# Reading the convolution's transposed value from PSUM, and the inverse root of the norms as one GpSimd power

## The reference

```
x = x + tanh(g_xattn[0]) * conv_mix(layernorm(x), ctx)      # stage A
x = x + tanh(g_ffn[0])   * moe_ffn(layernorm(x))            # stage B
x = x + tanh(g_xattn[1]) * attention(layernorm(x), ctx)     # stage C
x = x + tanh(g_ffn[1])   * lora_moe_ffn(layernorm(x))       # stage D

layernorm(x) = (x - mean(x)) / sqrt(var(x) + 1e-5)

# conv_mix, with v = layernorm(x), 16 heads of 8 rows each:
kv  = v[i] * ctx[j]                  # all 8 x 8 pairs of rows of a head
y   = causal_conv(kv, k[head]) + kv * bias
out = sum over i of y[i, j] * ctx[i]
```

## Time and profile before

| | us |
|---|---|
| median of 3 runs | 895.25 |
| lowest and highest of them | 890.1, 895.4 |
| the profiled execution, its whole time | 886.02 |
| its span in the trace | 884.3 |
| PE busy in the span | 787.3 |
| DVE busy | 618.5 |
| ACT busy | 319.5 |
| POOL busy | 171.2 |

### The profile page before, as it was taken

How to read it: one execution, slowest core, us unless ns; L and a number is a source line. 1 busy time by engine, 2 the same in 40 slices (tenths; PEclk the granted TensorE clock), 3 DMA queues, 4 the chain that set the end, 5 groups by cost and what they waited for, 6 DMA issues and landing times.

```text
span 884.3 us, 13802 instructions
## 1 busy us (share of the span) xinstructions
PE 787.3 (89%) x4627; PEld 629.2 (71%) x4627; DVE 618.5 (70%) x1196; ACT 319.5 (36%) x515; POOL 171.2 (19%) x185
## 2 busy tenths in 40 slices
PE   2887879699999999999997999976699999999994
PEld 2565657478888888888885455535588878888884
DVE  5999999754575466457546888897446785877764
ACT  2120212033333342342233777756143323334221
POOL 1999989700000000003000121211010000000000
PEclk9999999999999999999999999998589999999998
DMA  7221212000000000000101112110000000000000
GB/s 274 72 71 61 75 47 65 13 1 1 1 1 0 0 0 0 0 0 20 31 1 44 51 54 85 53 42 13 0 1 1 1 24 0 0 24 0 24 1 25
DMA packets 22133, 26.06 MB, mean 29 GB/s; under 512 B 5328, under 2 KB 17744, under 8 KB 21968
## 3 DMA queue, kind: packets, MB, share of 16 engines
q1 hardware_dynamic: 22096, 25.60, 9.2%
HBM read 23.22 MB, written 2.10 MB: 29 GB/s over the span
## 4 chain that ended last, share of the span: by engine, by line
PE 67%; DVE 20%; issue 8%; ACT 3%; POOL 1%; DVEq 1%; DMA 1%; SPq 0%; ACTq 0%; POOLq 0%
PE bank L1592 21%; PE bank L1460 19%; PE bank L1473 11%; PE bank L1523 2%; DVE A L864 2%; DVE A L875 2%; PE bank L1513 2%; DVE small L1071 1%; PE bank L1376 1%; PE bank L1601 1%; PE bank L1533 1%; DVE A L1081 1%; PE bank L1510 1%; PE bank L1377 1%; PE bank L1378 1%
## 5 line engine op out<-in xcount | busy, mean ns | idle before, releaser
L1592 PE MATMUL bank<-R 128*128 128x512 f32 (+3 forms) x1080 | 214.9, 360 | 11.4 <-DVE R L1235 4.9
L1592 PEld LDWEIGHTS bank<-R 128*128 128x128 f32 (+1 forms) x1080 | 180.8, 190 | 45.0 <-DVE R L1235 5.1
L1460 PE MATMUL bank<-R 128*128 128x512 f32 x768 | 186.2, 392 | 1.9 <-issue 1.9
L1460 PEld LDWEIGHTS bank<-R 128*128 128x128 f32 x768 | 140.4, 188 | 29.3 <-issue 2.2
L1019 DVE TENSOR_TENSOR A<-bank,A 128x512 f32<-128x512 f32 (+1 forms) x68 | 47.1, 692 | 113.1 <-PE bank L1460 110.8
L1473 PEld LDWEIGHTS bank<-R 128*128 128x128 f32 (+1 forms) x816 | 105.8, 190 | 10.5 <-issue 4.0
L1473 PE MATMUL bank<-R 128*128 128x256 f32 (+1 forms) x816 | 109.4, 284 | 2.5 <-DVE R L1029 2.2
L579 ACT ACTIVATE A<-bank 128x512 f32<-128x512 f32 (+1 forms) x68 | 40.6, 597 | 189.2 <-PE bank L1460 181.5
L1376 PE MATMUL bank<-A 128*128 128x256 f32 x128 | 45.1, 436 | 25.8 <-DVE A L864 17.6
L451 POOL TENSOR_TENSOR A<-A 128x256 f32<-128x256 f32 x64 | 64.1, 1001 | 10.3 <-DVE A L875 10.3
L1376 PEld LDWEIGHTS bank<-A 128*128 128x128 f32 x128 | 21.8, 202 | 44.7 <-DVE A L864 24.9
(11 more groups left out here) (172 smaller groups left out, 1129.4 us busy)
## 6 DMA issues: line engine op xcount, KB each, us to landing
A<-in_w SPq DMA_DIRECT2D x16, 384.0 KB, 3.0
A<-in_w SPq DMA_DIRECT2D x8, 480.0 KB, 3.6
A<-in_ctx_one SPq DMA_DIRECT2D x8, 272.0 KB, 3.6
A<-in_ctx_half SPq DMA_DIRECT2D x8, 256.0 KB, 3.1
A<-in_ctx_nat SPq DMA_DIRECT2D x4, 512.0 KB, 3.7
A<-in_ctx_t SPq DMA_DIRECT2D x128, 16.0 KB, 2.0
out<-X SPq DMA_DIRECT2D x4, 512.0 KB, 2.9
A<-in_filt SPq DMA_DIRECT2D x1, 1536.0 KB, 11.8
```

Of the source, the lines that this page charges most:

```text
L1460: mm = nc.tensor.matmul(dst[0:pr], wX[:, j, at + k * P:at + k * P + pr], mX[:, k], start=(n == 0), stop=(n == 5))
L1592: mm = nc.tensor.matmul(dst, a, m, start=start and n == 0, stop=stop and n == len(prods) - 1, skip_group_check=skip)
```

## The change

1. **The transposed value stays in PSUM.** `a_turned` and vT are gone. a_kv reads TV itself. TV is now two PSUM tiles, bank[2] for even and bank[1] for odd groups, and WB shares bank[3] with OB. The transposition of group g+1 therefore waits for the multiplications of group g-1, the block sums wait for an earlier a_finish, and a_sum waits for a_skip.
2. **The kv ring has four buffers instead of two (KVS), and a_kv runs three heads ahead instead of two (AHEAD).** PE puts three convolutions of the next group ahead of a_sum instead of two.
3. **The inverse root is made by POOL.** After bn_aggr, POOL adds epsilon (128x4 or 128x12) and raises to the power -0.5 in one instruction each. DVE waits for `rs_ready`, multiplies the gain in where there is one (one instruction), and makes nb. The guess and the Newton rounds are gone.
4. **a_skip** of the next group comes at head 11 instead of at head 16.
5. The group loops of stage A on DVE and PE are written out instead of run as hardware loops.

```diff
-TURN_A, BIAS_A = 6, 8
+TURN_A, BIAS_A, SKIP_A = 6, 8, 11
+AHEAD, KVS = 3, 4
...
-        TV, WB, OB = bank[1], bank[2], bank[3]
+        TV, OB = [bank[2], bank[1]], bank[3]
+        WB = OB
...
+            def inverse_root(seen, rs, mv):
+                pool.wait_ge(var_ready, seen)
+                root.mark(nc.gpsimd.tensor_tensor(rs, mv[:, :, 1], eps[:].to_broadcast([P, rs.shape[1]]), ALU.add))
+                pool.wait_ge(root_step, root.value())
+                nc.gpsimd.tensor_tensor(rs, rs, minus_half[:].to_broadcast([P, rs.shape[1]]), ALU.pow).then_inc(rs_ready, 1)
...
+            def a_adds(g, norm):
                 for c in range(CH - len(SPLIT_AT)):
                     split_low(g, c)
                 for h in range(NH0):
                     a_add(g, h)
+                    if norm and h == NORM_A + 3:
+                        inverse_root(BG * (g + 3), rs[:], mv)
                     if h in SPLIT_AT:
                         split_low(g, CH - len(SPLIT_AT) + SPLIT_AT.index(h))
+            for g in range(2):
+                inverse_root(BG * (g + 1), rs[:], mv)
...
+            start = root.value()
+            with pool.Fori(0, G - 1) as g:
+                root.enter(g, 1, start)
+                inverse_root(BG * (G + 2) + BG * g, rs[:], mv)
+            root.leave(1, G - 1, start)
...
+            inverse_root(2 * B + B - BG, crs[:, 0:B - BG], cmv[:, 0:B - BG])
+            inverse_root(3 * B, crs[:, B - BG:], cmv[:, B - BG:])
...
+            split_low1(G - 1, 0)
+            inverse_root(4 * B - BG, drs[:, 0:B - BG], dmv[:, 0:B - BG])
+            split_low1(G - 1, 1)
+            inverse_root(4 * B, drs[:, B - BG:], dmv[:, B - BG:])
...
-            def a_turned(g, first=False):
-                act.wait_ge(vtp_ready, g + 1)
-                if not first:
-                    act.wait_ge(kv_ready, NH0 * g)
-                for k in range(DT):
-                    nc.scalar.activation(vT[:, k * BG:(k + 1) * BG, :], TV[:, k * NT:(k + 1) * NT], ACT.Copy
-                                         ).then_inc(vT_ready, 1)
...
                     step.mark(nc.vector.bn_stats(st[:, i, :], x(i)))
-                    return
-                i -= n
-                if i == 0 or i > n:
+                elif i == n:
                     dve.wait_ge(dve_step, step.value())
-                if i == 0:
-                    step.mark(nc.vector.memset(scrap[:], 0.0))
-                elif i <= n:
-                    step.mark(nc.vector.bn_aggr(mv[:, i - 1, :], st[:, i - 1, :]))
-                elif i == n + 1:
-                    step.mark(nc.vector.tensor_scalar(ve, mv[:, :, 1], EPS, None, ALU.add))
-                elif i == n + 2:
-                    step.mark(nc.vector.tensor_scalar(rs.bitcast(I32), ve.bitcast(I32), 1, None,
-                                                      ALU.logical_shift_right))
-                elif i == n + 3:
-                    step.mark(nc.vector.tensor_scalar(rs.bitcast(I32), rs.bitcast(I32), -1, RSQRT_GUESS,
-                                                      ALU.mult, ALU.add))
-                elif i < n + 4 + 4 * NEWTONS:
-
-                    newton, part = divmod(i - n - 4, 4)
-                    if part == 0:
-                        step.mark(nc.vector.tensor_tensor(tmp, rs, rs, ALU.mult))
-                    elif part == 1:
-                        step.mark(nc.vector.tensor_tensor(tmp, tmp, ve, ALU.mult))
-                    elif part == 2:
-                        step.mark(nc.vector.tensor_scalar(tmp, tmp, -0.5, 1.5, ALU.mult, ALU.add))
-                    elif newton == NEWTONS - 1 and gain is not None:
-                        step.mark(nc.vector.scalar_tensor_tensor(out=rs, in0=rs, scalar=gain, in1=tmp,
-                                                                 op0=ALU.mult, op1=ALU.mult))
+                    nc.vector.memset(scrap[:], 0.0)
+                elif i < 2 * n + 1:
+                    i -= 1
+                    nc.vector.bn_aggr(mv[:, i - n, :], st[:, i - n, :]).then_inc(var_ready, 1)
+                elif i == 2 * n + 1 and gain is not None:
+                    dve.wait_ge(rs_ready, turn)
+                    step.mark(nc.vector.tensor_scalar(rs, rs, gain, None, ALU.mult))
+                else:
+                    if gain is None:
+                        dve.wait_ge(rs_ready, turn)
                     else:
-                        step.mark(nc.vector.tensor_tensor(rs, rs, tmp, ALU.mult))
-                else:
+                        dve.wait_ge(dve_step, step.value())
...
-                u = h % 2
+                u = h % KVS
                 t0 = h * I0
                 c = ctxT[:, h // 8, :, t0 % 64:t0 % 64 + I0]
+                v = TV[g % 2][:].rearrange("p (q t) -> p q t", t=P)
 
                 if not first:
-                    dve.wait_ge(y_ready, 1 + NH0 * g + h - 1)
+                    dve.wait_ge(y_ready, 1 + NH0 * g + h - AHEAD)
                 nc.vector.tensor_tensor(
-                    kv[:, u], vT[:, :, t0:t0 + I0].unsqueeze(3).to_broadcast([P, 8, I0, I0]),
+                    kv[:, u], v[:, :, t0:t0 + I0].unsqueeze(3).to_broadcast([P, 8, I0, I0]),
                     c.unsqueeze(2).to_broadcast([P, 8, I0, I0]), ALU.mult).then_inc(kv_ready, 1)
...
-                    if more and h == NH0:
+                    if more and h == SKIP_A:
...
-            with dve.Fori(0, G - 2) as g:
-                step.enter(g, per, start)
+            for g in range(G - 2):
...
-                if not first:
-                    pe.wait_ge(vT_ready, 2 * g)
+                if g > 1:
+                    pe.wait_ge(kv_ready, NH0 * (g - 1))
...
+                    pe.wait_ge(a_done, 1 + 2 * (g - 1))
...
-                pe.wait_ge(a_done, 1 + 2 * g)
+                pe.wait_ge(t_done, min(g + 2, G))
...
-            with pe.Fori(0, G - 1) as g:
-                for h in range(2, NH0):
+            for g in range(G - 1):
+                for h in range(2 if g == 0 else LEAD, NH0):
                     a_conv(g, h)
                     if h == TURN_A:
                         a_turn(g + 1)
                     if h == BIAS_A + 2:
                         a_block_sums(g + 1)
-                for h in range(2):
+                for h in range(LEAD):
                     a_conv(g + 1, h)
                 a_sum(g)
```

More of the change, by code:

```diff
@@ L437, in _ @@
             c.mark(nc.gpsimd.tensor_copy(identb[:], ident[:]))
+            root = Count(root_step)
+            def inverse_root(seen, rs, mv):
[3 more added lines that the diff above has]
+                nc.gpsimd.tensor_tensor(rs, rs, minus_half[:].to_broadcast([P, rs.shape[1]]), ALU.pow).then_inc(rs_ready, 1)
             def split_low(g, c):
@@ L463, in a_adds @@
                     a_add(g, h)
+                    if norm and h == NORM_A + 3:
+                        inverse_root(BG * (g + 3), rs[:], mv)
                     if h in SPLIT_AT:
                         split_low(g, CH - len(SPLIT_AT) + SPLIT_AT.index(h))
+            for g in range(2):
+                inverse_root(BG * (g + 1), rs[:], mv)
+            start = root.value()
             with pool.Fori(0, G - 1) as g:
-                a_adds(g)
-            a_adds(G - 1)
+                root.enter(g, 1, start)
+                a_adds(g, True)
+            root.leave(1, G - 1, start)
+            a_adds(G - 1, False)
             for c in range(CH, J0 - CH * (G - 1)):
                 split_low(G - 1, c)
+            start = root.value()
+            with pool.Fori(0, G - 1) as g:
+                root.enter(g, 1, start)
+                inverse_root(BG * (G + 2) + BG * g, rs[:], mv)
+            root.leave(1, G - 1, start)
             pool.wait_ge(h_ready, 1 + J0 * (G - 1))
@@ L904, in a_heads @@
                 route = Steps() if more else group_route(0)
+                if more and g < G - 2:
+                    norm_of = lambda: group_norm(g + 2, gate[:, 0:1])
+                elif more:
+                    norm_of = lambda: group_norm(0, None)
                 for h in range(LEAD, NH0 + LEAD if more else NH0):
@@ L1276, in _ @@
             norm = group_norm(1, gate[:, 0:1])
-            norm.take(2 * BG + 1)
+            norm.take(BG)
             dve.wait_ge(vN_ready, BG)
             norm.take_all()
-            dve.wait_ge(vT_ready, 2)
+            dve.wait_ge(vtp_ready, 1)
             dve.wait_ge(ctxT_loaded[0], 16)
-            for h in range(2):
+            for h in range(AHEAD):
                 a_kv(0, h, True)
@@ L1286, in _ @@
                 a_z(0, h, h < 2)
-                a_kv(0, h + 2)
+                a_kv(0, h + AHEAD, h + AHEAD < KVS)
                 if h == 1:
@@ L1291, in _ @@
             dve.wait_ge(small_loaded, 16 * 3)
-            per = N_STATS + 1
-            start = step.value()
-            with dve.Fori(0, G - 2) as g:
-                step.enter(g, per, start)
+            for g in range(G - 2):
                 a_heads(g, True)
                 a_finish(g)
```

(5 more changed lines are left out.)

70 lines of the change are left out of this document (31 added, 39 removed).

## The result

| | before | after |
|---|---|---|
| median, us | 892.69 (890.1 to 895.4, 4 runs) | 878.13 (875.75 to 878.37, 4 runs) |
| the profiled execution, whole time | 886.02 | 878.24 |
| its span | 884.3 | 876.5 |

A forecast was written before the change was run, and what follows sets the result against it. DVE was taken to set stage A's rounds, PE stage B. Rounds 15.3, last group 2.7, start 2.5, C and D 3 sum to 23.5; 895.25 less 23.5, less 1.75 for the profiled run's distance, gives 870 us, range 853 to 886.

The forecast's parts named there:

- a_kv from PSUM: Stage A on DVE: a_kv takes 679 ns without waits; all 8.7 us of waiting go, 2.0 of it per round.
- The Newton steps: Round of stage A on DVE: fourteen norm steps go, 7.2 us in all.
- Head 11: Round of stage A: a_skip stands between a_kv and z(12), so PE waits 2.1 us.
- Clock: Round of stage A: a low-clock stretch costs about 1.7 us of PE time; half counted, 0.8.
- Last group: Last group of stage A: the rest of a_kv's waiting goes, 2.7 us gained.
- C and D: Leaving out ten steps at C's start and ending the 12-wide chain before POOL's weight part gain 3 us together.
- C's start: Start of stage C: DVE first waits for the root, about 0.7 us more.
- Rival 3: The power takes over 4 us, so the kernel is slower, 945 at 10 us; chance 0.09.
- rival 4: First power call at the start is dear: 871 to 874 us, or 876 by the skill's figure; chance 0.09.
- rival 5: Stage A: a_kv keeps its waits or the broadcast PSUM read is slower, 8.7 us less gained, 879; chance 0.05.
- Rival 1: Stage A: engines unlock better, round about 29.5 us, 9 us less, 861; chance 0.16.
- Rival 2: The power takes 1.5 to 3.5 us, costing 5.5 us per us up to about 1.9, then 8.5; chance 0.15.

The follow-up runs named there:

- experiment 5: Changed kernel with Newton rounds on DVE instead of the power, and a kv ring of two buffers, two heads ahead: 882.18 us, ratio 0.9866.
- experiment 1: Two kernels: changed kernel with Newton rounds on DVE again, 877.94 us, ratio 0.9842; kernel before with only the power on POOL, 889.88 us, ratio 0.9974.
- experiment 7: The changed kernel run once more, unaltered: 876.0 us, ratio 0.9832.
- experiment 3: Changed kernel with nb of D's 12-wide norm written after the last score block's DVE work: 872.35 us, ratio 0.9788.
- experiment 6: Changed kernel with norms' last steps later in A, C, D: 867.96 us; also with skip split 865.93, each power twice 873.15, skip at head 13 873.12.
- experiment 2: Changed kernel with each power made twice, once into a scratch tile: 889.57 us, ratio 0.9977.

## Why the prediction came out as it did

The time lies in the range and 8 us above the number. The cause of the gain was right, the sum that priced it was not. Point by point:

- **a_kv from PSUM.** Right in size: 655 to 692 ns in all 64, and the root of the gain. It was priced at 8.7 in all, from a_kv's own excess; experiment 5 shows 10 to 12 from it, the skip's place and the loops, and POOL's adds and the small steps are quicker too.
- **The Newton steps.** The largest step that failed is "Fourteen norm steps go ... 7.2 in all", added to the 2.0 of a_kv as if the two were independent. By experiment 1 removing the steps alone shortens a round by 0.3 and with a_kv out of the way they cost 3.3 of DVE. The sum for DVE's round (27.9 forecast, 27.1 measured) was nearly right (fourteen overlaps of 0.08 would make it 28.1), but the parts of it were not: a stretched instruction's time belongs to the pair that contends, and went over to a_kv, the next one that met POOL's adds.
- **"DVE sets the round".** Half right. POOL's 34.4 busy us were read and not used as a second bound. In the power-only kernel POOL is busy 35.3 of 37.4.
- **The power, 0.7 us.** Measured 1.02, and 2.27 for 12 wide, for which the sum had no term of its own; by the prediction's own sign (L445 over 2 us) the wide ones are a miss. The wait in front of the gain was 1.59 (forecast 1.2) and PE's 2.50 (1.9).
- **Head 11.** Right: 2.1 forecast, 1.88 and 2.05 measured. Another wait of 0.88, for z(14) ahead of the next group's first convolution, was not seen.
- **Clock.** 0.8 a round was allowed. It is nothing in one round and 1.5 in another of the same trace. With the longer waits, rounds are 33.4 and 34.9 instead of 32.6: 11.1 gained, not 15.3.
- **Last group, 2.7.** 0.4 measured, but that takes two clocks together. PE's wait for POOL there is old (2.73 before, 3.18 now); a_sum runs 5.47 us instead of 3.84 because of the lower clock (experiment 7). In the trace with the skip at head 16, the one other at full clock, the last group takes 31.3 us and the gain is 2.0, and so it is between the changed kernel and the power-only one (35.0), both at 0.74. The term was about right, and the clock hid it.
- **Start 2.5 and stage B 0.** Both right: from the last a_finish to the last b_finish both traces take 300.1 us.
- **C and D, 3 gained.** Not borne out: -6.3 in the traces, and the 6.3 is mostly clock. The step was "the chain is now over before that part starts". It is over, but at 12 wide its root takes 2.27 + 0.21 on POOL, nb waits in front of DVE's softmax steps, and PE's 4.85 of idle time follows. That is 1.6 of it (experiment 3); the steps of C before it gain 0.9. Another 1.2 (the last step of C, clock 0.50 against 0.67) and 3.1 (D's start, 0.50 against 0.66) are PE at a lower clock. The 3.1 comes and goes in the same kernel (experiment 7) and is no effect of the change; for the 1.2 (4.36 and 3.65 in two traces of the changed kernel, 3.13 before) that is open.
- **C's start, "+0.7".** 1.3 lost, which closes the 6.3. DVE does wait 1.34 there, but the kernels of experiment 6, in which it does not, lose the same (322.8 us from A's end to the first c_finish, 321.45 before), and the kernel without a power loses 1.9. The traces show PE at a granted clock of 0.87 in that stretch against 1.00 before. No other trace has 1.00 there (0.79 to 0.92 from the last b_finish on), with or without a power. Why it falls there stays open.
- **The rivals.** Rival 3 (over 4 us), rival 4 (first call dear; the first power took 1.02) and rival 5 are out. Rival 1's round of 29.5 was not reached even with the later places (31.3 to 31.8 at full clock). Rival 2's size was nearly that of the 12-wide power, and its slope of 5.5 us per us is too low: experiment 2 has 11.4 for 1 us more on 128x4 and 2.3 more on 128x12. That stage B pays once the root is past about 1.9 us came true (1.0 in both kernels with the power twice).

By the medians the gain is 14.6 instead of 23.5, 8.9 short; in the traces it is 7.8, 15.7 short. The 6.7 between the two is the quick execution of before, and the forecast was right to start from the timed runs (893.5). As an estimate from the traces above, with the stretches left out that differ only in clock, 4.2 of the 8.9 are missing in the rounds, 0.7 in the last group and 3.7 in C and D (0.9 gained and 1.6 lost where 3 was forecast). That the forecast's DVE sum came within 0.8 of the measured one was luck: experiment 1 puts the steps at 3.3 where 7.2 was forecast, and the PSUM read at 6.1 (36.5 to 30.4) where it was 2.0.

## What to carry to other kernels

Where two engines stretch each other's instructions, do not subtract a removed instruction at its stretched time; find the pair that contends and change where one of them reads. A step handed to another engine costs its wait, so write the waiting instruction behind everything that a third engine needs: that alone took the changed kernel from 0.984 to 0.971. Look at the widest case of a moved operation, not the commonest. And before a loss is read from two single traces, compare the granted clock of the same stretch in both: here that was most of the 6.3.

## What the hardware did that was not expected

- The power on GpSimd takes 1.02 us for 128x4 and 2.27 for 128x12; a line through the two would be 0.16 us for each element of a partition and 0.4 beside it (an estimate from two sizes). An addition of 128x4 and 128x12 takes 0.20 and 0.21.
- A small DVE step of 128x4 that is all in SBUF still stretches beside POOL's adds: the gain takes 0.69 in the rounds, where it ends within 0.03 us of the add beside it, and 0.23 at the start, where POOL is idle.
- PE's granted clock was 0.50 to 0.56 behind 3.5 us of idle time in each of three rounds, and behind 2.5 us 0.54 in one round and 1.00 in the next. The start of D took 13.96 us at 0.50 in one execution of the changed kernel and 11.10 at 0.69 in another.
